# Two column orders for a cast: the bf16 copy of the queries is read and written first in the even columns and then in the odd ones

## What is computed

```python
# wide layer (0 and 2)
q, k, v = x @ Wq, ctx @ Wk, ctx @ Wv          # 16 heads of 64
logits = einsum(q, k) * 64 ** -0.5 + col_bias # bias from two masks, on 4 of 154 keys
x = x + softmax(logits) @ v @ Wo + bo
# narrow layer (1 and 3)
xn = x * rsqrt(mean(x * x) + eps) * norm_w
q, k, v = xn @ wq, ctx @ wk, ctx @ wv         # 16 query heads of 16, 4 key heads
x = x + softmax(einsum(q, k) * 16 ** -0.5) @ v @ wo
```

## Time and profile before

| | before |
|---|---|
| median of 3 runs | 1703.9 us (1693.34 to 1705.22) |
| the profiled execution | 1708.63 us |
| its span on the core | 1706.8 us |
| PE busy | 1569.7 us (92%) |
| DVE busy | 1259.1 us (74%) |
| ACT busy | 1015.4 us (59%) |
| POOL busy | 496.6 us (29%) |

### The profile page before, as it was taken

How to read it: one execution, slowest core, us unless ns; L and a number is a source line. 1 busy time by engine, 2 the same in 40 slices (tenths; PEclk the granted TensorE clock), 3 DMA queues, 4 the chain that set the end, 5 groups by cost and what they waited for, 6 DMA issues and landing times.

```text
span 1706.8 us, 29380 instructions
## 1 busy us (share of the span) xinstructions
PE 1569.7 (92%) x10491; PEld 874.2 (51%) x10604; DVE 1259.1 (74%) x2325; ACT 1015.4 (59%) x1721; POOL 496.6 (29%) x368
## 2 busy tenths in 40 slices
PE   7898788999999999999989999999999999999875
PEld 7787535454545454554445454545454545454432
DVE  5483566787877887888878788778788878787652
ACT  2111265667676666766666767576766667676443
POOL 5342402132232322232223223222332222323231
PEclk9898899999999999999999999999999999999988
DMA  8998413150315031513253223313250316031422
GB/s 274 319 336 234 151 24 65 38 99 25 77 42 131 23 84 36 130 33 86 64 129 93 66 53 88 96 30 74 54 120 21 83 38 135 24 84 23 126 71 83
DMA packets 176737, 160.56 MB, mean 94 GB/s; under 512 B 91722, under 2 KB 133066, under 8 KB 175570
## 3 DMA queue, kind: packets, MB, share of 16 engines
q1 hardware_dynamic: 174154, 149.95, 34.2%
q10 hardware_dynamic: 2440, 8.73, 1.3%
HBM read 115.11 MB, written 43.48 MB: 93 GB/s over the span
## 4 chain that ended last, share of the span: by engine, by line
PE 42%; issue 17%; DVE 11%; POOL 8%; ACT 4%; SPq 4%; DMA 3%; ACTq 0%; POOLq 0%; DVEq 0%
PE general L1706 8%; PE general L1587 7%; PE score_ps L1647 5%; POOL kept L1433 4%; PE score_ps L1646 4%; PE out_ps L1661 3%; PE general L1608 3%; PE out_ps L1682 3%; DVE a_lo L1523 2%; PE general L1604 2%; SPq L1085 2%; DVE q_aux L1478 2%; PE score_ps L1635 2%; PE general L1666 2%; PE out_ps L1672 2%
## 5 line engine op out<-in xcount | busy, mean ns | idle before, releaser
L1487 DVE TENSOR_REDUCE tops<-general 128x2 bf16<-128x308 f32 x1024 | 428.1, 470 | 48.5 <-PE general L1604 24.1
L1298 ACT ACTIVATE probs<-score_ps 128x512 f32<-128x512 f32 x512 | 294.8, 597 | 133.4 <-PE score_ps L1647 125.9
L1433 POOL TENSOR_TENSOR kept<-kept,inv_b 128x512 f32<-128x512 f32 x128 | 172.4, 1369 | 509.4 <-DMA inv_b<-scratch_inverses 488.0
L1474 DVE TENSOR_TENSOR q_pair<-general,q_pair 64x512 fp32r<-64x512 f32 x160 | 109.5, 684 | 163.1 <-ACT q_pair L1286 159.8
L1310 ACT ACTIVATE q_aux<-general 4x512 bf16<-4x512 bf16 x320 | 187.6, 586 | 16.9 <-PE general L1617 11.7
L1285 ACT ACTIVATE q_pair<-general 64x512 fp32r<-64x512 f32 x160 | 94.6, 591 | 133.8 <-PE general L1587 103.8
L1355 ACT ACTIVATE a_hi<-kept 128x512 fp32r<-128x512 f32 x160 | 93.5, 623 | 95.3 <-PE general L1706 60.0
L1647 PE MATMUL score_ps<-q_pair,w_pair 128*128 128x512 f32 x256 | 148.8, 586 | 0.0
L1523 DVE TENSOR_TENSOR a_lo<-kept,a_hi 128x512 fp32r<-128x512 f32 x160 | 129.3, 841 | 23.4 <-ACT a_hi L1355 22.6
L1322 ACT ACTIVATE kept<-out_ps 128x512 f32<-128x512 f32 x192 | 104.2, 595 | 70.4 <-PE general L1676 54.3
L1647 PE MATMUL score_ps<-q_pair,n_pair 128*128 128x512 f32 x256 | 144.5, 582 | 0.2 <-ACT probs L1298 0.2
(11 more groups left out here) (164 smaller groups left out, 3245.9 us busy)
## 6 DMA issues: line engine op xcount, KB each, us to landing
inv_b<-scratch_inverses SPq DMA_DIRECT2D x128, 256.0 KB, 4.8
w_pair<-scratch_wk_hi SPq DMA_DIRECT2D x32, 256.0 KB, 6.9
x<-scratch_stream SPq DMA_DIRECT2D x16, 512.0 KB, 3.5
inv_n<-scratch_inverses SPq DMA_DIRECT2D x248, 32.0 KB, 1.8
xn<-scratch_stream SPq DMA_DIRECT2D x15, 512.0 KB, 3.4
scratch_stream<-x SPq DMA_DIRECT2D x14, 512.0 KB, 4.1
scratch_wk_hi<-p_kout_hi SPq DMA_DIRECT2D x16, 308.0 KB
p_raw<-in_L_xattn_Wk_dram SPq DMA_DIRECT2D x4, 1024.0 KB, 7.0
```

The lines of the kernel that those rows point to most:

```text
L1298: nc.scalar.activation(dst, score_ps[:, number % 2, :], ACT.Exp, scale=scale).then_inc(act_exp.sem, 1)
L1433: last = nc.gpsimd.tensor_tensor(tiles[i], tiles[i], (inv_b, inv_n)[n % 2][:, i, :], ALU.mult)
L1487: last = nc.vector.tensor_reduce(tops[:, n % 2, sub, 2 * pair:2 * pair + 2], src, AX_X, ALU.max)
```

## The change

Only the access patterns of the two casts change. Each cast covered 512 adjacent columns of a row; now it goes through the row as two rows of 256 columns each, first the columns 0, 2, 4, ..., then 1, 3, 5, .... Source and destination are walked in the same order, so every value lands where it did. In the program the innermost step is 2 elements (8 bytes in `q_pair`, 4 bytes in `q_aux`) and the outer step is 1 element. Number, place, partitions, types, waits and signals of the instructions stay as they were, and DVE has the same 1321 rows in its program.

```diff
                     last.then_inc(dve_query.sem, 1)
-                    nc.vector.tensor_copy(q_aux[0:64, t, s, j, :], q_pair[0:64, s, j, :])
-                    nc.vector.tensor_copy(q_aux[64:P, t, s, j + 1, :], q_pair[64:P, s, j + 1, :]).then_inc(dve_aux.sem, 1)
+                    def apart(row):
+
+                        return row.rearrange("p (a b) -> p b a", b=2)
+
+                    nc.vector.tensor_copy(apart(q_aux[0:64, t, s, j, :]), apart(q_pair[0:64, s, j, :]))
+                    nc.vector.tensor_copy(apart(q_aux[64:P, t, s, j + 1, :]), apart(q_pair[64:P, s, j + 1, :])).then_inc(dve_aux.sem, 1)
```

## The result

The changed kernel takes 1710.1 us (median of 14 runs, 1703.1 to 1713.3), the kernel before 1703.2 us on the same chips (14 runs, 1693.3 to 1708.4). The ratio is 1.004, with a 95% interval of 1.0023 to 1.0057: 4 to 10 us slower, which is clear of chance and well within 1%. The profiled execution of the changed kernel has a span of 1706.3 us, no longer than the one before, so a pair of single executions could not have shown it; what the casts do can be read from it all the same.

A forecast was written before the change was run, and what follows sets the result against it. PE was taken as the bound, busy 92% of the span, with DVE next and about a fifth of its time free. The sum was 320 casts x 0 = 0, leaving the median at 1704 us; range 1692 to 1728 us.

The forecast's parts named there:

- The fast rate of the cast stays: Two DVE casts: splitting a row in two keeps two columns a tick, as L283 does; price 0.
- fallback to one column a tick without holding: Rival: casts take 0.69 us but no longer wait for POOL's instructions; -7 us, 1697 us, chance 0.07.
- The step of two columns costs 0: Two DVE casts: the column step adds 0, bounded above by 0.265 us more per cast at half rate.
- The two columns of a tick hinder each other: One reason given for the half rate: a tick's columns, now perhaps neighbours in memory, get in each other's way.
- half rate: Rival: casts take 0.69 us, still held by POOL; 15 to 21 us more, 1719 to 1725 us, chance 0.27.
- 58 to 80 of 320 casts are on the way to the end: Count of casts on the chain that ended last, 18 to 25%; only their growth was priced.
- quarter rate: Rival: casts take 1.22 us; 46 to 64 us more, 1750 us or above, chance 0.10.
- the other three in four casts are covered by PE's own queue; that cover is DVE's free fifth: Casts off the chain: DVE's free time would absorb growth, enough for 85 us more work.
- both slower rivals: Half rate, 1719 to 1725 us, chance 0.27, and quarter rate, 1750 us or above, chance 0.10.

The follow-up runs named there:

- writes alone: Against the kernel before, only the casts' writes go with a step of 2, reads in order; 1706.9 us, ratio 0.9997.
- pairs: Against the kernel before, casts walk neighbouring column pairs (0, 1, 4, 5, ..., then 2, 3, 6, 7, ...) on both sides; 1706.9 us, ratio 1.0013.
- halves outermost: Against the kernel before, casts take each half of 256 columns in turn, even columns first, then odd; 1709.4 us, ratio 1.0025.
- small copy ahead: Kernel before plus a DVE copy of 8 columns ahead of the two casts of each query entry; 1708.4 us, ratio 1.0019.
- cut in two: Kernel before with the first cast of each pair cut into columns 0 to 255 and 256 to 511, no step; 1721.3 us, ratio 1.0081.
- copy behind: Kernel before plus the same DVE copy of 8 columns behind the second cast of each query entry; 1725.7 us, ratio 1.0125.
- step 4: Against the kernel before, casts go in four walks with a step of 4 columns on both sides; 1767.4 us, ratio 1.0347.
- reads alone: Against the kernel before, only the casts' reads go with a step of 2, writes in order; 1706.4 us, ratio 1.0005.

## Why the prediction was right, and where it was not

**The fast rate of the cast stays.** Right. L283 with its two separate rows was the proper witness for splitting a row: the changed casts take 457 ns, not 690. The fallback to one column a tick without holding did not happen, since the maxima are still 1565 and 2534 ns.

**The step of two columns costs 0.** The forecast of 1704 us was right to 0.4%, but this term was mis-sized: it is 37 ns a cast at the median and 13.1 us over all casts, against a bound of 265 ns a cast. The runs split it in two. A write of single bf16 values every 4 bytes costs some 35 ns a cast (writes alone 453 and 459 ns, pairs 421 and 425). A read of every second word costs nothing by itself (420 and 425 ns), but a cast with such reads gets longer by up to 0.14 us where it lies over the wide layers' small products of PE. In the kernel before that meeting was free, so no row of it could have shown the price; that such an overlap exists could have been read. What in these products does it stays open: those of the narrow layers have the same form and leave the cast alone.

By the prediction's estimate from the Trainium skill, Vector Engine (DVE) Microarchitecture Reference (Measured stream behaviour on trn2), a cast that reads lone 4-byte words would take 0.59 us or more; the trace has 420 ns for reads with a step of 8 bytes, so that rule does not hold down to this step. The Trainium skill, SBUF — State Buffer (the note on cachelines), asks for two hits in each 16 bytes; the trace agrees for the reads, and with 752 ns at a step of 16 bytes in its direction. But by that rule the write with a step of 4 bytes would be free too, and the trace has it at 453 ns. The measurement decides.

**The two columns of a tick hinder each other.** That reason for the half rate falls with the run that has halves outermost: 458 and 461 ns, as with the change.

**58 to 80 of 320 casts are on the way to the end.** As a factor for small growth this is 18 to 25%. It fits the small copy ahead, the halves and the writes alone, and is below the lower ends for the change (3.9 of 13.6 us is 0.29), the cut in two and the copy behind (0.38 and 0.40). As a factor for the half rate it was too low: the sum gave 15 to 21 us for 85 us of casts, where step 4 passes on 59 of 108 us, which by the same share would be some 47 us for 85, an estimate. The sum for the quarter rate, 46 to 64 us for casts of 1.22 us, was much too low as well: with 1.33 us the end moved by 237 us. The prediction had seen that more casts would then come on the chain, but its "1750 us or above" named no upper end. So the step "the other three in four casts are covered by PE's own queue; that cover is DVE's free fifth" failed. It held back the price of both slower rivals. That the range held in spite of it is luck as far as this step goes: had the half rate come, which the prediction gave 27 in 100, the same estimate puts the end near 1751 us, outside the 1728 us of the range. It did not matter because the casts grew by only 13 us in all.

Why the change passed on half of its 13.6 us, and the small copy ahead only a fifth of 16.6 us, stays open. Their intervals in us overlap (3.9 to 9.7 and 0.5 to 6.0), and no run here tells chance from a cause. That the delay of the signal `dve_aux` is all that counts (Theory G) is excluded by the two small copies: the run that leaves the signal alone is the slower one.

## What to carry to other kernels

A busy share says how much time an engine has free, not where. Here DVE was busy 82% at most in any stretch of the main part, and still about half of 46 us and of 108 us added to it reached the end, and five sixths of 282 us, by when it was as busy as PE. The count of instructions on the chain gave a factor of about a fifth, which only some of the small doses bear out. On an engine that is coupled to the bound at many places, price a rival with a larger dose by half or more of the added time.

A column step of two in a cast from f32 to bf16 keeps the fast rate and costs 9% at the median, 8% of it by the write. With pairs of columns kept together it costs nothing at the median. Steps of four and eight on both sides make the same cast 1.8 and 3.2 times as long.

Where two engines are both close behind the bound, try moving part of a job before all of it: one of the two casts on ACT gave 0.7%, both cost 1.8%.

## What the hardware did that I had not expected

A cast that reads every second word took 0.50 to 0.59 us in place of 0.42 to 0.46 us where it lay wholly over the wide layers' small products of PE (26 such casts after the change and 22 with reads alone; before, 28 such casts took 419 to 427 ns). So a DVE instruction can get longer over work of PE, and it depends on the pattern that DVE uses. Over the narrow layers' products of the same form, of which eight start together in place of twelve, it stayed at 451 to 457 ns (12 casts) and, with reads alone, 420 to 425 ns (11 casts). Whether it is the number, PE's reads or something else was not tested. Moving probs_rest by 24 KB left it (26 casts wholly over the wide products, 508 to 562 ns).

Two DVE instructions that work on the same 64 partitions can overlap: the cast behind the small copy started 0.07 us after the copy's start, which lasts 0.16 us, and behind the first half of the split cast (0.29 us) the second started after 0.21 us:

```profile
242.14 0.29 DVE L1477 CAST q_aux<-q_pair 64x256 bf16<-64x256 f32 x1
242.35 0.28 DVE L1478 CAST q_aux<-q_pair 64x256 bf16<-64x256 f32 x1
242.64 0.42 DVE L1479 CAST q_aux<-q_pair 64x512 bf16<-64x512 f32 x1
```

The third, on the other 64 partitions, started when the second had ended. The Trainium skill, VectorE: DVE Perf Modes (Two Vector instructions with no wait between them), has it so: an instruction whose operands start in another group of 32 partitions than the last ones is held until all before it are done. The trace agrees: from start to start it is 0.21 us in one case, less than the 0.29 us of the first half, and 0.29 us in the other, as long as the second half took with the gap behind it.
